# Two graph attention layers on one Trainium2 core: three signals of TensorE instead of one, offsets loaded between weighings, POOL's second bias moved to VectorE

## The reference, cut to what matters

```python
def gat_conv(x, src, dst, W, a_src, a_dst, b):
    h = (x @ W).reshape(N, HEADS, HEAD_DIM)            # 8 heads of 32
    alpha_s = jnp.einsum('nhc,hc->nh', h, a_src)
    alpha_d = jnp.einsum('nhc,hc->nh', h, a_dst)
    e = alpha_s[src] + alpha_d[dst]
    e = jnp.where(e > 0, e, NEG_SLOPE * e)
    m = jax.ops.segment_max(e, dst, num_segments=N)
    ex = jnp.exp(e - m[dst])
    denom = jax.ops.segment_sum(ex, dst, num_segments=N)
    alpha = ex / (denom[dst] + 1e-16)
    msg = h[src] * alpha[:, :, None]
    return jax.ops.segment_sum(msg, dst, num_segments=N).reshape(N, 256) + b
...
h = jax.nn.elu(gat_conv(x, src, dst, W1, a_src1, a_dst1, b1))
out = gat_conv(h, src, dst, W2, a_src2, a_dst2, b2)
...
x = x + _L1_gnn_ref(_layernorm(x, axis=-1), edge_index, ...)
```

## Time and profile before

| What | us |
|---|---|
| median of 3 runs | 2844.16 |
| lowest, highest | 2842.58, 2845.69 |
| the profiled execution's own time | 2847.07 |
| its span, first to last instruction | 2845.3 |
| busy: PE, PEld | 1964.8, 1543.5 |
| busy: DVE, POOL, ACT | 1638.5, 1434.1, 992.5 |

### The profile page before, as it was taken

The page is one execution under the profiler, slowest core; times in us unless marked ns, Lnnn a source line. Parts: engine busy times, 40 slices in busy tenths (PEclk is TensorE's granted clock), DMA queues, the critical chain, the costliest instruction groups (busy, mean ns, idle before and its releaser), DMA issues.

```text
span 2845.3 us, 38141 instructions
## 1 busy us (share of the span) xinstructions
PE 1964.8 (69%) x10306; PEld 1543.5 (54%) x10306; DVE 1638.5 (58%) x5066; ACT 992.5 (35%) x2446; POOL 1434.1 (50%) x1424
## 2 busy tenths in 40 slices
PE   7999776666775999963656565556255566564699
PEld 5888544444464999952444444444144444443377
DVE  5200233333357555573777777777387777877544
ACT  4444100000011444424445454443344454442422
POOL 1100477777721343314776667623776766661343
PEclk9999877767666999986778888787588787877599
DMA  5444433333345999963444444411444444440000
GB/s 210 195 192 194 144 104 105 104 105 105 104 108 186 357 350 358 341 211 121 131 131 121 117 126 131 123 51 47 132 136 119 131 124 118 124 118 9 0 23 24
DMA packets 187233, 400.48 MB, mean 141 GB/s; under 512 B 30958, under 2 KB 98098, under 8 KB 180558
## 3 DMA queue, kind: packets, MB, share of 16 engines
q0 software_dynamic: 63520, 179.35, 22.5%
q1 hardware_dynamic: 112270, 187.97, 18.5%
q10 hardware_dynamic: 11232, 30.68, 3.2%
HBM read 323.15 MB, written 75.54 MB: 140 GB/s over the span
## 4 chain that ended last, share of the span: by engine, by line
DVE 21%; PE 17%; issue 9%; DVEq 4%; POOL 3%; ACT 1%; DMA 0%; POOLq 0%; ACTq 0%; SPq 0%
PE banks L1473 5%; DVE arena L1559 4%; PE banks L1474 4%; DVEq L686 3%; DVE arena L1650 3%; POOL arena L1355 3%; DVE arena L1615 3%; PE banks L1444 2%; DVEq L689 1%; PE banks L2027 1%; PE banks L2029 1%; PE banks L2028 1%; PE banks L1314 1%; DVE arena L1661 1%; DVE nrmT L1602 1%
## 5 line engine op out<-in xcount | busy, mean ns | idle before, releaser
L1355 POOL DMA_INDIRECT arena<-ht,srcT x784 | 792.9, 1011 | 408.4 <-issue 223.1
L722 POOL DMA_INDIRECT arena<-tr,idx1T x392 | 374.9, 956 | 327.1 <-DMA tr<-arena 207.9
L750 PE MATMUL banks<-arena 128*128 x884 | 341.0, 537 | 164.8 <-SPq L729 148.7
L1473 PE MATMUL banks<-arena,XT 128*128 128x264 f32 x884 | 361.8, 499 | 98.1 <-DVE arena L1650 69.4
L750 PEld LDWEIGHTS banks<-arena 128*128 128x128 f32 x884 | 215.0, 263 | 290.5 <-issue 257.8
L1474 PE MATMUL banks<-arena,XT 128*128 128x264 f32 x884 | 335.5, 468 | 0.0
L1650 DVE TENSOR_TENSOR arena<-arena,nrmT 128x528 f32<-128x528 f32 x448 | 311.8, 700 | 30.6 <-ACT nrmT L1420 30.6
L1473 PEld LDWEIGHTS banks<-arena,XT 128*128 128x128 f32 x884 | 207.7, 248 | 158.8 <-DVE arena L1650 75.1
L1398 ACT ACTIVATE arena<-iorow,dlT 128x128 bf16<-128x128 f32 x896 | 267.9, 387 | 65.4 <-issue 65.2
L411 PE MATMUL banks<-parts 128*128 128x512 f32 x1200 | 275.2, 391 | 4.7 <-DVE parts L371 4.7
L773 DVE TENSOR_TENSOR X<-X,banks 128x256 f32 x221 | 91.5, 414 | 312.1 <-PE banks L750 311.3
(11 more groups left out here) (356 smaller groups left out, 3292.9 us busy)
## 6 DMA issues: line engine op xcount, KB each, us to landing
arena<-in_L_ffn_w_dram SPq DMA_DIRECT2D x195, 512.0 KB, 6.0
tr<-arena SPq DMA_DIRECT2D x50, 1024.0 KB, 3.9
XT<-dld ACTq DMA_DIRECT2D x52, 512.0 KB, 4.2
arena<-ht,srcT POOLq DMA_INDIRECT x784, 2.8
ht<-arena SPq DMA_DIRECT2D x50, 136.0 KB, 1.8
arena<-ys SPq DMA_DIRECT2D x10, 640.0 KB, 5.6
arena<-tr,idx1T POOLq DMA_INDIRECT x392, 2.8
arena<-in_L_gnn_weight_dram SPq DMA_DIRECT2D x8, 512.0 KB, 8.9
```

What stands on the lines that cost most here:

```text
L722: pool.indirect_dma_start(Gr[:, o:o + D], None, TR, bass.IndirectOffsetOnAxis(ap=idx1T[:, q:q + 1], axis=0)).then_inc(d_g[b % NG], 16)
L750: mm = ten.matmul(B[n][:, 0:D], OHr[:, n, h, :], Gr[:, h * D:][:, bass.ds(o, D)], start=(h == 0), stop=(h == 1))
L1355: pool.indirect_dma_start(Gall[:, o:o + ROW], None, HT[L], bass.IndirectOffsetOnAxis(ap=srcT[:, q:q + 1], axis=0)).then_inc(d_g[b % NG], 16)
L1473: ten.matmul(B[n][:, 0:MSG], OH[b][:, 2 * j, :], WG[:, j, 0, :], start=True, stop=False)
```

## The change

**Signals.** `half_ok` and `turn` are gone. `scores` raises `sc_ok`, `expand` raises `spread_ok`, and `pr_ok`, so far raised by the first four products alone, is raised by both halves. Each reader waits for that of the three which it reads: the scan for `sc_ok`, the second four additions and the widening for `pr_ok`, the tables, the weights and the transfer of the places for `spread_ok`.

**Offsets.** The load ahead of the rescaling (`ao_`) goes between the second and third weighing, that ahead of the tables (`tb_`, now for the next chunk) between the fourth and fifth, and that of the maxima (`mo_`), so far between the sixth and seventh, to the start of `values`.

**Second bias.** POOL only clears the sums. VectorE adds the bias in five instructions in the second layer's loop at i = -2, ahead of the first scan. ScalarE's loop between the layers is written in another way, with the same order of instructions. The semaphore `hd4_ok` becomes a higher count of `nm_ok`.

```diff
             if c > 1:
-                eng.wait_ge(half_ok, turn(L, c - 3))
+                eng.wait_ge(spread_ok, L * NCH + c - 1)
...
-                    act.wait_ge(half_ok, turn(L, c - 4))
+                    act.wait_ge(sc_ok, L * NCH + c - 1)
...
-                    act.wait_ge(half_ok, turn(L, c - 2))
+                    act.wait_ge(pr_ok, 2 * (L * NCH + c - 1))
...
                     t = ten.transpose(B[7][0:8 * CH, n * P:(n + 1) * P], AS[c % 2][:, n * 8 * CH:(n + 1) * 8 * CH], ident[:, :])
-                return t
+                t.then_inc(sc_ok, 1)
...
                 if q_on:
-                    last = scores(q)
+                    scores(q)
                 if n_on:
                     to_.load(n * CH)
                 if c_on:
-                    last = products(c, 4, 8)
+                    products(c, 4, 8).then_inc(pr_ok, 1)
                 if n_on:
-                    last = expand(n)
-                last.then_inc(half_ok, 1)
+                    expand(n).then_inc(spread_ok, 1)
...
             def tables(c):
-                k = L * NCH + c
-                tb_.load(c * CH)
...
-                    vec.wait_ge(half_ok, turn(L, c - 2))
+                    vec.wait_ge(spread_ok, L * NCH + c)
...
                     if j < 4:
-                        ins.wait_op(pr_ok, L * NCH + c + 1, "sem-ge")
+                        ins.wait_op(pr_ok, 2 * (L * NCH + c) + 1, "sem-ge")
                     else:
-                        ins.wait_op(half_ok, turn(L, c), "sem-ge")
+                        ins.wait_op(pr_ok, 2 * (L * NCH + c + 1), "sem-ge")
...
-                vec.wait_ge(half_ok, turn(L, c - 2))
+                vec.wait_ge(sc_ok, L * NCH + c + 1)
                 vec.tensor_tensor_scan(SC, rep[c % 2], B[7][0:8 * CH, 0:EW], -BIG, ALU.add, ALU.max).then_inc(scan_ok, 1)
...
-                vec.wait_ge(half_ok, turn(L, c - 1))
+                vec.wait_ge(spread_ok, L * NCH + c + 1)
...
+                    if j == 1:
+                        ao_.load(c * CH)
+                    if j == 3 and c + 1 < NCH:
+                        tb_.load((c + 1) * CH)
                     yield
...
             def open_sums(c):
-                ao_.load(c * CH)
...
                 weave(across(q) if q_on else none())
+                if L and i == -2:
+                    for g in range(NGR):
+                        t = slice(g * GT, g * GT + GT)
+                        vec.tensor_tensor(X[:, t, :], X[:, t, :],
+                                          bb2[1].rearrange("p (o c) -> p o c", o=1).to_broadcast([P, GT, D]), ALU.add)
...
                 pool.memset(ACC[:, t0 * MSG:(t0 + GT) * MSG], 0.0)
-                pool.tensor_tensor(X[:, t0:t0 + GT, :], X[:, t0:t0 + GT, :],
-                                   bb2[1].rearrange("p (o c) -> p o c", o=1).to_broadcast([P, GT, D]), ALU.add)
```

More of the change, by code:

```diff
@@ L1286, in build @@
         pm_ok, p2_ok, pj_ok, one_ok = (sem(n) for n in ("pm_ok", "p2_ok", "pj_ok", "one_ok"))
-        as_ok, half_ok, scan_ok, back_ok, sm_ok, sb_ok, mx_ok, vv_ok, sp_ok, ee_ok, x_in, x_ok = (sem(n) for n in (
-            "as_ok", "half_ok", "scan_ok", "back_ok", "sm_ok", "sb_ok", "mx_ok", "vv_ok", "sp_ok", "ee_ok", "x_in", "x_ok"))
+        as_ok, spread_ok, scan_ok, back_ok, sm_ok, sb_ok, mx_ok, vv_ok, sp_ok, ee_ok, x_in, x_ok = (sem(n) for n in (
+            "as_ok", "spread_ok", "scan_ok", "back_ok", "sm_ok", "sb_ok", "mx_ok", "vv_ok", "sp_ok", "ee_ok", "x_in", "x_ok"))
         w_ok, f_in, f_ok, pr_ok, ad_ok, ob_ok, oh_ok, ot_ok = (sem(n) for n in (
             "w_ok", "f_in", "f_ok", "pr_ok", "ad_ok", "ob_ok", "oh_ok", "ot_ok"))
-        nm_ok, el_in, el_ok, hd4_ok, at_ok = (sem(n) for n in ("nm_ok", "el_in", "el_ok", "hd4_ok", "at_ok"))
+        sc_ok = sem("sc_ok")
+        nm_ok, el_in, el_ok, at_ok = (sem(n) for n in ("nm_ok", "el_in", "el_ok", "at_ok"))
         def block_at(at):
             return Gall[:, bass.ds(at, 2 * ROW)].rearrange("p (a c) -> p a c", a=2)
-        def turn(L, i):
-            return L * (NCH + 2) + i + 3
         def steps_of(c):
@@ L1594, in values @@
                 pm = B[6][:, 0:25 * CH].rearrange("p (s c) -> p s c", c=25)
+                mo_.load(c * CH)
                 vec.wait_ge(mx_ok, k + 1)
@@ L1607, in values @@
                 yield
-                mo_.load(c * CH)
                 state["max"] = after_own(vec.tensor_copy(Mo, M[:, bass.ds(mo_.at(c * CH), 8)]), state["max"])
@@ L1667, in dve_gat @@
             dv.n += 1
+            tb_.load(0)
             for i in range(-2, NCH):
@@ L1717, in act_second_layer, with exps @@
             go = act_project(1)
-            for g in range(NGR + 1):
-                if g < NGR:
-                    act.wait_ge(el_in, g + 1)
-                    act.activation(O2[g % 3], O[g % 3], ACT.Exp).then_inc(el_ok, 1)
-                if g:
-                    for i in range((g - 1) * GT, g * GT):
-                        act_turned(ELU, i)
-                        if i > 1:
-                            go(i - 2)
+            def exps(g):
+                act.wait_ge(el_in, g + 1)
+                act.activation(O2[g % 3], O[g % 3], ACT.Exp).then_inc(el_ok, 1)
+            exps(0)
+            for i in range(NT):
+                if i % GT == 0 and i // GT + 1 < NGR:
+                    exps(i // GT + 1)
+                act_turned(ELU, i)
+                if i > 1:
+                    go(i - 2)
             for i in (NT - 2, NT - 1):
@@ L1826, in attend @@
                             vec.wait_ge(at_ok, t - 2)
-                        dve_heads(t, hd4_ok)
+                        dve_heads(t, nm_ok)
                 vec.wait_ge(at_ok, g + 1)
@@ L1852, in attended @@
                 t0 = g * GT
-                pool.wait_ge(hd4_ok, g + 1)
+                pool.wait_ge(nm_ok, NGR + g + 1)
                 pool.tensor_tensor(X[:, t0:t0 + GT, :], X[:, t0:t0 + GT, :], O[g % 3], ALU.add).then_inc(at_ok, 1)
```

## The result

| | us |
|---|---|
| after, median of 4 runs | 2757.68 |
| lowest, highest | 2742.49, 2762.31 |
| before, in the same comparison | 2844.93 |
| after / before | 0.969, 95% interval 0.966 to 0.972 |
| the profiled execution, its span | 2757.96, 2756.2 |

A forecast was written before the change was run, and what follows sets the result against it. POOL's gathers were taken to bound the attention layers after the change: 62 us a layer, 124 in two, plus 8 for the second bias, 132 us off, so 2712 us, range 2688 to 2752.

The forecast's parts named there:

- The scan's wait: VectorE's idle time before the scan, 1.69 us a step, goes wholly, since the scan needs only the transposed scores.
- the additions' own input: Second four additions: late next is the fourth product's end; they need not wait for the spread any more, 1.48 us.
- The loads: VectorE's offset loads: 0.6 and 0.45 us a chunk saved, three loads among the weighings at 0.1 us each added.
- the 0.3 us allowed: Sign on VectorE: eight weighings take as long as before within 0.3 us; more means the loads are not hidden.
- The chain: Step through ScalarE and TensorE, additions to additions: 18.2 us against 20.96, with the first product at +14.5 and products of 3.64.
- So POOL sets the end: POOL's gathers, 18.7 us a chunk against the chain's 18.2, end the layer some 10 us later than the chain alone.
- The clock: TensorE's clock falling between products in some steps of the attention layers: 1 us taken off the gain.
- rival 3: Slower: second products at TensorE's lower clock, 7.04 us instead of 3.64, deciding from 81% of chunks; 2863 us, chance 0.04.
- The second bias: Between the layers: moving POOL's five additions to VectorE saves 7.8 us, between 5.2 and 13.3.
- the 7.5 feared: VectorE's five bias additions might hold one gather each for 1.49 us, 7.5 us on the stream; nothing was taken.
- The upper end of the range: 2752 us, from gathers all at the weighing stretch's pace: 41 us a layer and 8, given as 92 off 2844.
- Rival 2: Half the gain: loads cost as before among the weighings, only 1.4 us of the scan's wait goes; 2761 us, chance 0.22.

The follow-up runs named there:

- g1: Changed kernel with TensorE's register load of the sums' places ahead of the scores, not between scores and second products: 2726.9 us, ratio 0.959.
- h4: Changed kernel with the second gather of each block left out from block 25 on, 221 gathers a layer instead of 392: 2757.6 us.
- f4: Changed kernel with the second bias back on POOL between the layers: 3328.4 us, where the unaltered changed kernel takes 3299.7.

## Why the prediction was wrong, step by step

- **The scan's wait: right.** It is gone, wholly, but for the first chunks. What comes next was named as well (the additions' own input), but not that it would be waited for at every chunk.
- **The loads: right in size, small in worth.** Eight weighings span 5.28 us from first to last start (1595.51 to 1600.79) against 5.14 before, inside the 0.3 us allowed. The rescaling and the tables (now L1659, L1526) lost their idle time (medians of 0.03 and 0 us instead of 0.67 and 0.45), and VectorE can do 18.3 us a step, as g1's quickest steps show.
- **The chain: mis-sized in one term, too short by 0.5 us.** "Now the first product waits 0.35 us for an addition": the profile named L1559 as the releaser, and I believed it. After the change that addition (L1554 at 1583.18, 0.43 us) is over 0.89 us before the product starts, and the 0.34 us are still there. It was TensorE's own register load, as g1 shows by moving it. The slow step above has its scores 14.21 us behind the additions (14.11 predicted), the product at 14.96 (14.5), and the additions 0.20 us behind the start of the spread. With 3.64 us of products that is 18.8 us, not 18.2.
- **"So POOL sets the end": wrong.** h4 takes the gathers' load off and nothing moves, and the score copies, forecast to idle for landed blocks in most chunks, did so 7 times in both layers. The pace of 18.7 us that I drew from them was right by accident, since the true chain has the same length.
- **The clock: the step that failed.** I took off 1 us a layer and gave the clock, as rival 3, 0.04, with the argument that the products of the earlier trace rows ran at the high level right after 2.48 us of idle time and that the change lengthens no pause. It shortens it, to 1.3 us in many chunks, and the slow products went from 13 to 26. Each slow step is 2.07 us longer than a fast one (20.73 - 18.66), 26 x 2.07 = 54 us, where 2 were planned; 54 steps of 18.7 us would be 1010 us instead of the measured 1061.5, 52 us less. That is the whole shortfall, and a little more. Rival 3 was priced all or nothing, at 3.4 us and from 81% of the chunks; half of the chunks at 1.7 us never came up. I had read one chunk of before; a count over all would have shown 13 slow chunks, and where they stand: eight behind pauses of 2.53 us and more, and five in all the chunks with pauses of 1.43 to 1.49 us, while the 39 others have 1.69 to 2.59 us. The shorter pause was no safe ground in the trace of before.
- **The second bias: right in kind, too small.** 7.8 us predicted. From scan to scan it is 12.1 us less (116.1 to 104.0), but 2.2 of these lie in the first layer's last chunks; from its last addition to the next layer's first gather it is 11.7 us less, to the first scan 9.9 (81.2 to 71.3). On another chip, with only the bias moved, it is 11.9 from scan to scan. L1713 takes its 0.82 us each time, as announced, but ScalarE's pace is 5.7 us a group, not the 7.0 that I read between two L1721 which POOL still delayed. By an inference of the Trainium skill (SBUF — State Buffer, "Who interferes with whom") a tensor_tensor takes only the read side and leaves descriptor generation, which needs the write side, alone. The trace agrees less well: beside the five additions six gathers took 1.09 to 1.88 us instead of 0.95, together 1.9 us lost, less than the 7.5 feared. (In f4, without these additions, one gather at that place takes 1.29 us too, so up to 0.36 us isn't theirs.) The first scan idles 14.71 us, 12.5 expected.
- **The upper end of the range** adds 2 x 41 + 8 us to 92; it is 90, so 2754 us instead of 2752, and the result lies above either.
- **Rival 2 has the number, 2761 us, and not the mechanism.** It blamed loads among the weighings and a scan wait that remained; neither is there.

## What to carry to other kernels

Once a signal is split, the work that it used to cover is on the path, so read how that work varies over all its instances, not in one. A short load of registers between two groups of matmuls costs its own time and, here, in half of the chunks, the clock of what follows; place it ahead of the wait that precedes both. And before a term is called the bound, ask what would be idle if it weren't: taking 44% of the gathers away answered that in one run.

## What the runs showed of the hardware

- In the changed kernel the second products took 3.6 or 5.3 us and nothing between (5.9 us in the first chunk of a layer), and which of them a chunk gets goes with differences of 0.05 to 0.1 us in the pause ahead. Moving one register load out of the place between scores and products cut the count of those over 4.5 us from 30 of 52 to none on one chip and from 13 of 52 to none on another; where VectorE never idles long, it is 12 of 52 instead of 26, on two chips.
- Eight extra matmuls a chunk in TensorE's idle time made the kernel 30 us slower with the mean granted clock of a 400 us stretch hardly changed (0.79 and 0.80), and fourteen made the kernel before 49 us slower on another chip.
- The same kernel takes 2844 us on some chips and 3393 to 3410 on others. There VectorE waits 12 us in most chunks of the attention and 23 us in every 34 of the relational gather stage, and in the attention this goes with the traffic of the gathers (407.9 us in 39 waits with all of them on one chip, 32.2 us in 10 with 44% left out on another). What it waits for the traces don't name, and it wasn't tried further.
